# Layer 2 of a two-layer LoRA block: from one level of seven products to two, with GpSimd making one operand's inner sums

## The reference, cut to what matters

```python
# x: (8, 512, 2048); L0 weight: (8, 2048, 2048); L1 W: (2048, 2048), b: (2048,)
# lora_As: (32, 2048, 16), lora_Bs: (32, 16, 2048)
x1 = x + einsum('bsi,boi->bso', x, L0_weight[itok_B_3_7])       # layer 1
h  = einsum('bti,bir->btr', x1, lora_As[itok_B_0_23])
y  = x1 + einsum('bti,oi->bto', x1, W) + b \
        + einsum('btr,bro->bto', h, lora_Bs[itok_B_0_23]) * 2.0  # layer 2
```

## Time and profile before

| | |
|---|---|
| median of 3 runs | 2774.69 us (2774.22 to 2776.67) |
| profiled execution | 2774.51 us, its span 2772.9 us |
| TensorE busy | 2707.6 us (98%), 11904 matmuls |
| VectorE, ScalarE, GpSimd busy | 1281.4, 605.0, 393.8 us |
| granted TensorE clock, mean | 0.993 |
| moved by DMA | 644.76 MB, 233 GB/s on average |

### The profile page before, as it was taken

The page is one execution under the profiler, slowest core; times in us unless marked ns, Lnnn a source line. Parts: engine busy times, 40 slices in busy tenths (PEclk is TensorE's granted clock), DMA queues, the critical chain, the costliest instruction groups (busy, mean ns, idle before and its releaser), DMA issues.

```text
span 2772.9 us, 29633 instructions
## 1 busy us (share of the span) xinstructions
PE 2707.6 (98%) x11904; PEld 2236.8 (81%) x11904; DVE 1281.4 (46%) x1656; ACT 605.0 (22%) x785; POOL 393.8 (14%) x738
## 2 busy tenths in 40 slices
PE   7999999999999999999997799999999999999998
PEld 6888888888888888888886588888888888888886
DVE  4454454454544545445442544455343644455442
ACT  3232242332322323323220111010101111011100
POOL 2111111111111111111113002210121101210010
PEclk9999999999999999999999899999999999999999
DMA  7565555566655656555549558895788758895674
GB/s 259 205 221 182 197 209 203 207 216 204 213 201 200 207 201 220 187 204 208 181 144 370 195 203 287 288 365 198 251 286 338 270 205 287 278 376 196 225 241 171
DMA packets 140829, 644.76 MB, mean 233 GB/s; under 512 B 19604, under 2 KB 19604, under 8 KB 104852
## 3 DMA queue, kind: packets, MB, share of 16 engines
q1 hardware_dynamic: 69556, 370.19, 38.2%
q0 software_dynamic: 71136, 272.68, 27.3%
HBM read 506.47 MB, written 136.31 MB: 232 GB/s over the span
## 4 chain that ended last, share of the span: by engine, by line
PE 93%; DVE 2%; DMA 2%; issue 1%; POOL 1%; ACT 0%; SPq 0%; DVEq 0%; POOLq 0%; ACTq 0%
PE bank L628 17%; PE bank L630 16%; PE bank L629 16%; PE bank L654 14%; PE bank L657 14%; PE bank L655 14%; DMA hs<-h_mix 1%; DVE bank L542 1%; PE bank L613 1%; PE bank L614 1%; PE bank L668 1%; POOL c_sum L267 1%; DVE xc L551 0%; DMA w_raw<-w0T 0%; PE bank L675 0%
## 5 line engine op out<-in xcount | busy, mean ns | idle before, releaser
L628 PE MATMUL bank<-x_hi,w_hi 128*128 128x512 f32 x2048 | 797.7, 390 | 16.6 <-DVE x_lo L454 16.6
L630 PE MATMUL bank<-x_hi,w_lo 128*128 128x512 f32 x2048 | 797.2, 389 | 0.0
L629 PE MATMUL bank<-x_lo,w_hi 128*128 128x512 f32 x2048 | 797.2, 389 | 0.0
L654 PE MATMUL bank<-xc,wl 128*128 128x512 f32 x1792 | 700.3, 391 | 40.1 <-DVE xc L551 23.3
L655 PE MATMUL bank<-xc,wl 128*128 128x512 f32 x1792 | 698.6, 390 | 0.0
L657 PE MATMUL bank<-xc,wl 128*128 128x512 f32 x1792 | 698.4, 390 | 0.0
L628 PEld LDWEIGHTS bank<-x_hi,w_hi 128*128 128x128 f32 x2048 | 384.8, 188 | 97.5 <-issue 16.3
L336 ACT ACTIVATE w_hi<-w_raw 128x1024 fp32r<-128x1024 f32 x256 | 257.5, 1053 | 935.9 <-PE bank L630 925.3
L630 PEld LDWEIGHTS bank<-x_hi,w_lo 128*128 128x128 f32 x2048 | 384.7, 188 | 80.0
L629 PEld LDWEIGHTS bank<-x_lo,w_hi 128*128 128x128 f32 x2048 | 384.8, 188 | 79.8
L654 PEld LDWEIGHTS bank<-xc,wl 128*128 128x128 f32 x1792 | 337.3, 188 | 115.1 <-DVE c_sum L572 17.3
(11 more groups left out here) (54 smaller groups left out, 1364.3 us busy)
## 6 DMA issues: line engine op xcount, KB each, us to landing
wl<-w1s SPq DMA_DIRECT2D x224, 1024.0 KB, 5.5
w_raw<-w0T SPq DMA_DIRECT2D x256, 512.0 KB, 5.8
w1s<-q_out POOLq DMA_DIRECT2D x56, 1024.0 KB, 6.2
x1s<-x_raw POOLq DMA_DIRECT2D x128, 256.0 KB, 2.3
c_sum<-x1s POOLq DMA_DIRECT2D x128, 256.0 KB, 5.8
yT<-c_sum POOLq DMA_DIRECT2D x128, 256.0 KB, 5.3
x_raw<-xT POOLq DMA_DIRECT2D x62, 512.0 KB, 4.4
q_raw<-w1T POOLq DMA_DIRECT2D x32, 512.0 KB, 9.3
```

The lines of the kernel that those rows point to most:

```text
L628: pe.matmul(sums[s][:], w_hi[s][:, k, :], x_hi[:, k, :], start=(k == 0), stop=False)
L629: pe.matmul(sums[s][:], w_hi[s][:, k, :], x_lo[:, k, :], start=False, stop=False)
L630: mm = pe.matmul(sums[s][:], w_lo[s][:, k, :], x_hi[:, k, :], start=False, stop=(k == KT - 1))
L654: pe.matmul(bank, w[:, 0, k, :], x[:, 0, :], start=(k == 0), stop=False)
```

## The change

Layer 2 works on groups of four batches, and each of the seven products of quadrants is itself made of seven products of quadrants of the quadrants: 49 inner products per group, 98 steps s in all (s = 7·outer + j). One step is four row blocks m, each with 4 x 3 matmuls. The outer sums of x1 are made in HBM during layer 1: beside `x1s`, each tile is written to, or added by an accumulating DMA into, up to three of five sum tensors `xss`; for what is subtracted ScalarE makes a negative copy `x1_neg`. The inner sums of x1 are made by GpSimd (`add_terms`), 128x2048 at a time in SBUF. ScalarE and VectorE split the result in two halves (`SPLITS`), into one of two buffers `xc`. The inner form adds some products up in PSUM over several steps, so that each step ends in one inner quadrant of one or two outer quadrants: one or two VectorE operations for each m (`INTO`).

The weights are prepared in 28 units of four tiles each: an outer sum 128x2048 on VectorE, four inner sums, seven splits, seven stores of 512 KB (196 in all), by n < 112. The LoRA's product and the bias no longer come with the last products: during tiles 4 to 11 of the next batch TensorE makes two 128x512 products a tile (`low_rank`), GpSimd loads the matching x1 tile (`xr`), VectorE adds all up (`add_lora`), and GpSimd stores the result (`cis`), from which `c_sum` starts. Those of the last batch come in steps 4, 5, 11 and 12 of layer 2. The h and B tensors in HBM (`hs`, `bs`) go. Layer 2's weights are loaded in pieces of 512 KB into five buffers, before in pieces of 1 MB into three.

```diff
+A_SUM = [(2, 0, ALU.subtract), (1, 3, ALU.subtract), (0, 3, ALU.add), (2, 3, ALU.add), (0, None, None),
+         (0, 1, ALU.add), (3, None, None)]
+S6, S7, S1, S3, S4 = range(5)
+B_SUM = [S6, S7, S1, None, S3, None, S4]
+B_PLAIN = [None, None, None, 0, None, 3, None]
+INTO = [((3, 1),), ((0, 1),), ((0, 1), (3, 1)), ((2, 1), (3, -1)), ((1, 1), (3, 1)), ((0, -1), (1, 1)),
+        ((0, -1), (2, -1))]
...
+BEGINS = [(S1, S4, S6), (S3,), (S7,), ()]
+ADDS = [(), (S6,), (), (S1, S7)]
+SUBTRACTS = [(), (), (S4,), (S3,)]
...
+INNER = 7
+IN_X = [True, False, True, False, True, True, False]
+BEGIN = [True, True, False, False, False, False, True]
+INNER_INTO = [0, 3, 1, 1, 3, 2, 0]
...
+PLACE = [0, 0, 0, 3, 1, 0, 2]
+BANK_BEFORE = [2, 2, 2, 2, 2, 1, 3]
+HAS_SUM = [False, True, True, False, True, True, False]
+SPLIT = [0, 6, 5, 1, 4, 2, 3]
+SPLIT_AT = [(0, 1), (2, 3), (4,), (5, 6)]
...
+            def load_q(u):
+                for i, quad in enumerate(unit_quads(u)):
+                    for row in range(2):
+                        tile = quad // 2 * HALF + row * Q + u % Q
+                        ks = slice(quad % 2 * HALF, quad % 2 * HALF + HALF)
+                        pool.dma_start(q_raw[i][:, row], w1T[tile, :, ks]).then_inc(q_loaded[i], 16)
+            def store_q(c):
+                u, i = divmod(c, INNER)
+                pool.wait_ge(q_ready, c + 1)
+                pool.dma_start(w1s[u // Q * INNER + SPLIT[i], u % Q], q_out[c % 2][:].bitcast(F32)
+                               ).then_inc(q_stored[c % 2], 16)
+            def load_xr(b, o):
+                i = b * NT + o
+                if i >= XR:
+                    pool.wait_ge(ci_stored[i % XR], i // XR * 16)
+                pool.dma_start(xr[i % XR][:], x1s[b, o]).then_inc(xr_loaded[i % XR], 16)
+            def store_ci(b, o):
+                i = b * NT + o
+                pool.wait_ge(ci_done, i + 1)
+                pool.dma_start(cis[b, o], xr[i % XR][:]).then_inc(ci_stored[i % XR], 16)
...
+            def add_terms(s):
+                if s >= SEQ or not HAS_SUM[s % INNER]:
+                    return
+                j, loads = s % INNER, (s // INNER + 1) * 16
+                into = xq[PLACE[j]][:]
+                if j == 1:
+                    pool.wait_ge(xq_loaded[1], loads)
+                    pool.wait_ge(xc_ready, s * SPLITS)
+                    pool.tensor_tensor(into, xq[1][:], into, ALU.subtract).then_inc(term_done, 1)
+                if j in (2, 4):
+                    pool.wait_ge(xq_loaded[3], loads)
+                    pool.wait_ge(xc_ready, s * SPLITS)
+                    pool.tensor_tensor(into, xq[3][:], into, ALU.subtract).then_inc(term_done, 1)
+                if j == 5:
+                    pool.wait_ge(xq_loaded[2], loads)
+                    pool.tensor_tensor(into, xq[2][:], into, ALU.subtract).then_inc(term_done, 1)
...
             for b in range(NB):
                 for t in range(NT):
                     n = b * NT + t
                     s = n % 2
+                    quad = t // HALF * 2 + b % 4 // 2
                     pool.wait_ge(x1_sum, n + 1)
                     pool.dma_start(x1s[b, t], x1_raw[s][:]).then_inc(x1_stored[s], 16)
+                    for i in BEGINS[quad]:
+                        pool.dma_start(xss[b // 4, i, b % 2, t % HALF], x1_raw[s][:]).then_inc(x1_stored[s], 16)
+                    for i in ADDS[quad]:
+                        pool.dma_start(xss[b // 4, i, b % 2, t % HALF], x1_raw[s][:],
+                                       accum_op=ALU.add).then_inc(x1_stored[s], 16)
+                    for i in SUBTRACTS[quad]:
+                        negatives += 1
+                        pool.wait_ge(x1_neg_done, negatives)
+                        pool.dma_start(xss[b // 4, i, b % 2, t % HALF], x1_neg[s][:],
+                                       accum_op=ALU.add).then_inc(x1_stored[s], 16)
                     if b < NB - 1 and t % KX == KX - 1:
                         load_x(b + 1, t // KX)
...
+                    if b > 0 and t in (0, 4):
+                        load_b(b - 1, t // 4)
...
+                    if b > 0 and t == LORA_FROM - 1:
+                        for o in range(2):
+                            load_xr(b - 1, o)
+                    for o in lora_tiles(b, t):
+                        if o + 2 < NT:
+                            load_xr(b - 1, o + 2)
+                    for o in lora_tiles(b, t):
+                        store_ci(b - 1, o)
+                    if n < UNITS * 4:
+                        for i in SPLIT_AT[n % 4]:
+                            store_q(n // 4 * INNER + i)
+                        if n % 4 == 3 and n // 4 + 1 < UNITS:
+                            load_q(n // 4 + 1)
+                    if n == TILES - 11:
+                        for i in range(2):
+                            pool.wait_ge(q_stored[i], UNITS * INNER // 2 * 16)
+                        load_xq(0, 0)
+                    if n == TILES - 2:
+                        pool.wait_ge(w_ready, TILES * PARTS)
+                        load_xq(0, 1)
+                        load_xq(0, 3)
+                        pool.wait_ge(tile_done, TILES - 1)
+                        load_xq(0, 2)
...
+            for i in (0, 3, 1, 2):
+                load_c(0, 3, i)
+            add_terms(1)
+            for i in (0, 3, 1, 2):
+                load_c(0, 0, i)
+            load_b(NB - 1, 0)
+            for o in range(XR):
+                load_xr(NB - 1, o)
+            for s in range(SEQ):
+                outer, j = divmod(s, INNER)
+                group, o = divmod(outer, OUTER)
+                if outer + 1 < SEQ // INNER and j in (3, 4, 5):
+                    pool.wait_ge(xc_ready, (s + 2) * SPLITS)
+                    for q in ((1, 3), (0,), (2,))[j - 3]:
+                        load_xq(outer + 1, q)
+                add_terms(s + 2)
+                if s == 4:
+                    load_b(NB - 1, 1)
+                late, first_tile = late_lora(s)
+                if late:
+                    for m in range(Q):
+                        store_ci(NB - 1, first_tile + m)
...
+                    i = INNER_INTO[j]
+                    if LAST[quad] == o and INNER_LAST[i] == j:
+                        b, t = place_of(group, quad, i)
+                        if group == 0:
+                            pool.wait_ge(acc_free, (s + 1) * Q)
+                            pool.dma_start(yT[b, t:t + Q].rearrange("t p n -> p t n"), c_sum[quad][:, i]
+                                           ).then_inc(y_stored[quad][i], 16)
+                if group == 1:
+                    for m in range(Q):
...
+            def xc_hi(s, h):
+                ks = slice(h * (Q // SPLITS), (h + 1) * (Q // SPLITS))
+                place = PLACE[s % INNER]
+                if s >= 2:
+                    act.wait_ge(acc_done, (s - 1) * Q)
+                if HAS_SUM[s % INNER]:
+                    act.wait_ge(term_done, xc_sums(s + 1))
+                else:
+                    act.wait_ge(xq_loaded[place], (s // INNER + 1) * 16)
+                act.activation(xc[s % 2][:, 0, ks], xq[place][:, ks], ACT.Copy).then_inc(xc_hi_done, 1)
...
@@ -365,6 +509,30 @@
                     else:
                         act.wait_ge(h_done, old_b + 1)
                 act.activation(x1_hi[s][:], x1_raw[s][:], ACT.Copy).then_inc(x1_hi_done, 1)
+                if n % NT >= HALF:
+                    act.wait_ge(x1_stored[s], x1_stores(n - 2) * 16)
+                    act.activation(x1_neg[s][:], x1_raw[s][:], ACT.Copy, scale=-1.0).then_inc(x1_neg_done, 1)
...
+            def add_lora(b, o, bank):
+                i = b * NT + o
+                dve.wait_ge(lora_done, i + 1)
+                dve.wait_ge(xr_loaded[i % XR], (i // XR + 1) * 16)
+                dve.scalar_tensor_tensor(out=xr[i % XR][:], in0=bank[:], scalar=bias_sb[:, o:o + 1],
+                                         in1=xr[i % XR][:], op0=ALU.add, op1=ALU.add).then_inc(ci_done, 1)
...
+            def split_q(n):
+                u, step = divmod(n, 4)
+                c = u * INNER
+                if step == 0:
+                    dve.wait_ge(q_loaded[0], q_load_count(u, 0) * 2 * 16)
+                    if len(unit_quads(u)) > 1:
+                        dve.wait_ge(q_loaded[1], q_load_count(u, 1) * 2 * 16)
+                        dve.tensor_tensor(q_raw[0][:], q_raw[0][:], q_raw[1][:], A_SUM[u // Q][2]).then_inc(q_added, 1)
+                    q_lo(c)
+                    q_lo(c + 1)
+                if step == 1:
+                    q_lo(c + 2)
+                    dve.wait_ge(q_ready, c + 3)
+                    dve.tensor_tensor(piece(3), piece(3), piece(2), ALU.add).then_inc(q_added, 1)
+                    q_lo(c + 3)
+                if step == 2:
+                    dve.tensor_tensor(piece(2), piece(0), piece(2), ALU.subtract).then_inc(q_added, 1)
+                    q_lo(c + 4)
```

(138 more changed lines are left out.)

462 lines of the change are left out of this document (135 added, 327 removed).

## The result

The changed kernel takes 2788.07 us (median of 5, 2787.55 to 2794.74) against 2774.69: ratio 1.0053, 95% interval 1.0038 to 1.0067. The prediction was 2632. The matmuls are as forecast, 11232 of them, and GpSimd's sums too. TensorE waits far more than forecast.

What follows compares the result with a forecast made beforehand. TensorE's list of matmuls was taken to bound the kernel. Terms -152.3 - 32 - 6.4 + 7 + 1.5 + 18 + 22 = -142.2 took 2772.9 to 2630.7, forecast 2632 us, range 2612 to 2655.

Steps and rivals of the forecast that it cites:

- Matmuls removed: Layer 2: 4704 matmuls in place of 5376, 672 fewer at 0.2266 us each, -152.3 us if nothing waits.
- G, and the steady steps: Layer 2: GpSimd's sum time G, taken as 4.9 us, costs nothing up to 7.0 us; 0 us.
- Rival 3: Layer 2: VectorE's low parts and GpSimd's sums hinder each other, 68 us more, 2700 us; chance 0.06.
- The turn: From layer 1 to layer 2: 5.5 us waiting and 1 us for the clock replace 38.5 us; -32 us.
- hidden, barely: Start of layer 2: step 2's sum is split by 28.7 us, against the need at 29; no cost.
- The late LoRA: Last batch's LoRA in layer 2: late x1 loads cost 6 us at step 6, 1 us at step 12; +7 us.
- The last chunk of x: Layer 1's seven batch turns: x's load 3.1 us later, less 0.5 us slack, 2.6 us each; +18 us.
- Layer 1's DMA: Layer 1: transfer queues delay six weight units (10 us) and x's chunk at three turns (12 us); +22 us.
- they may lag by 8 us at no cost: Layer 1: VectorE and ScalarE need 3.2 of 11.3 us for weight splits due one tile later, leaving 8 us.
- Rival 1: The DMAs bound layer 1: 64 us instead of 22, 2674 us, up to 2700; chance 0.17.
- The clock: TensorE's lower clock after idle time, priced at 1 us, at the turn to layer 2.

Runs made afterwards that it cites:

- Run 10: Changed kernel with x loaded first, three split-weight buffers, reordered layer 2, no weight work at t = 15, plus 128-column LoRA x1 tiles and results: 2644.30 us.
- Run 3: Changed kernel with the load of x's chunk issued ahead of the same tile's stores: 2735.26 us.
- run 4: Changed kernel with three buffers instead of two for layer 2's split weights on their way to HBM: 2745.45 us.
- run 7: Changed kernel with each of GpSimd's 56 sums made twice in a row: 2965.54 us.
- run 9: Same base kernel as Run 10, with plain writes for the 160 accumulating DMAs instead of the narrower LoRA transfers: 2643.13 us.
- Run 6: Changed kernel with layer 2 reordered: earlier B and x1 loads, earlier step 1 sum, h's low part first, LoRA in steps 4, 11, 18, 25: 2756.53 us.
- run 1: Changed kernel with layer 1's 160 accumulating DMAs made plain writes: 2733.06 us.
- run 2: Changed kernel with no outer sums of x1 (no DMAs into them, no negative copies), layer 2 reading x1 tiles instead: 2658.29 us.

## Why the prediction was wrong, point by point

In short, layer 1's transfers landed later than was taken, and TensorE's inputs stood behind them in the lists. Run 10 shows the first part (fewer bytes, same orders, 53 us), runs 3 and 4 the second (same bytes, other order or buffers, 53 and 43 us).

- **Matmuls removed, -152.3 us:** right in count and price.
- **G, and the steady steps, 0 us:** right. The sum takes 4.65 us (4.9 taken), it has the place that was worked out, and run 7 found the limit at about 7.3 on average (7.0). The Trainium skill's 4497 ns for this addition (GPSIMD Engine Reference, section 3.1 Elementwise) agrees within 4%.
- **Rival 3** did not cost its 68 us, because sums and low parts lie apart in the steady steps, 2117.9 to 2122.5 and from 2124.7 on. But its mechanism is in the trace. In step 94, near the end, GpSimd makes two sums in a row, and a low part falls into the second:

```profile
2736.78 4.63 POOL L338 TENSOR_TENSOR xq<-xq 128x2048 f32<-128x2048 f32 x1
```
```profile
2739.01 3.48 DVE L663 TENSOR_TENSOR xc<-xq,xc 128x1024 fp32r<-128x1024 f32 x1
```

  The low part takes 3.48 us instead of 1.22 and ends 1.1 us after the sum: it stood until GpSimd was done. The other 195 low parts touch no sum and take 1.21 to 1.23 us. TensorE waited 0.3 us for it. In run 9 a split of x1 of 0.69 us took 4.11 beside a sum, and in run 7 a sum took 5.40. The Trainium skill (SBUF — State Buffer, section Who interferes with whom) says that two such instructions contend. The trace agrees. VectorE's additions of a PSUM bank to one operand in SBUF keep their 0.69 us beside the sums (126 cases).
- **The turn, 5.5 us and 1 for the clock:** the shape was right, the sizes not. Step 1 waited 10.7 us, for h's low part, behind the first tiles of `c_sum` that landed 16 us after their issue; step 2, "hidden, barely", was hidden. Step 3 waited 5.9 us, for which the sum had no term: its split stands on ScalarE behind that of B, and ScalarE waited 20.6 us for B, whose load stood behind 8 MB. The late LoRA cost 17 us in two gaps instead of 7: a store to HBM took 8 to 9 us there, for which I had taken the 2.3 of an idle queue. Run 6 shows that all but the wait for `c_sum` are places in a queue.
- **The last chunk of x, +18 us:** right in mechanism, too small: the seven waits are 67.0 us. Its term "1 us" for the bytes ahead was 3 to 7, and 6 at the turn shown (11.5 us from issue to ScalarE instead of 5.4). Run 3 gained 53 us by this step's place alone.
- **Layer 1's DMA, +22 us:** this is the step that failed, together with the bytes in the term above: 40 us were priced for layer 1 and 164 lost. Beside the last chunk they are 51 us of waiting and 46 of lower clock. Three parts of the step failed. First, "they may lag by 8 us at no cost" has no room for a turn, where ScalarE and VectorE have seven chunks of x to split within one tile: five waits, 19.1 us. In the middle of a batch the lag itself was larger than taken, since a unit's 2 MB of W came 12 to 18 us after the first issue (11 to 13 taken): eight waits, 30.8 us. Secondly, the sum had no term for ScalarE waiting for the stores of its two buffers, 275 us in all (run 4: 43 us). Thirdly, I took durations from the kernel before, at a share of 0.61, and added the bytes ahead; at a share of 0.92 the store of 256 KB takes 5.5 us, a load of W 12.1.
- **Rival 1**, the DMAs, had the right mechanism and 0.17. It was bounded at 2700 because I let layer 1 be either limited by rate (546 MB at 354 GB/s, 1542 us) or not. It took 1640, which is 333 GB/s with the reads. How the engines' fixed order of waits makes them idle in turn is argued from the turn above, not measured by itself. Its cost was 1.0 to 1.3 us for each MB taken away (runs 1, 2, 9, 10), not the 2.8 us of a pure limit at 354 GB/s.
- **The clock:** 1 us was priced in all, 59 us were lost. Each longer gap is paid again behind it.

## What to carry to other kernels

When a change fills the DMA engines, durations from the emptier kernel don't hold: the 256 KB store of x1 took 2.3 us before, 4.9 at a share of 0.79 in layer 1 (run 2) and 5.5 at 0.92. Then list, for each engine, what stands behind each wait on a transfer at the tightest place of the schedule (here the turn of batch), and not the average slack. Issue the load that TensorE will wait for ahead of stores that are needed later. Count an accumulating DMA at twice its bytes, and price TensorE's gaps with the lower clock behind them. Keep VectorE's instructions with two operands in SBUF out of GpSimd's sums.

## What the runs showed of the hardware that I had not expected

- An accumulating DMA into HBM cost here about as much as twice its bytes in plain transfers (54.5 us for 42 MB of its reads, 53.3 us for 44 MB of plain ones, each to some 6 us). Its issue on GpSimd shows as 1.02 us, against 0.54 us for a plain one, and as 1.16 for those of the negative copies (0.54 when plain, run 1).
- Twenty gaps of TensorE of 1 to 12 us in layer 1 cost 46 us of lower clock beside 118 us of waiting. Between the two gaps shown above the price hardly differs. Behind the 5.1 us the granted clock was 0.50 (1.2 GHz) from 627.3 to 632.0, with a matmul each 0.43 us instead of 0.23, and 2.4 us were lost; behind the 11.6 us it was 0.50 from 651.0 to 655.5, and 2.5 us were lost. In the kernel before there were few such gaps, and the mean granted clock was 0.993 instead of 0.968. The Trainium skill (Advanced Engine Details and Errata, section Clock Domains) states that the array is gated to 1.2 GHz when idle. The granted clock of 0.50 behind the two gaps agrees.
- A VectorE instruction with two operands in SBUF stood until GpSimd's sum had ended (3.48 us instead of 1.22), as shown under rival 3.
